# Token shift and value blocks moved by DMA, and one mask product per chunk, in a two-block transformer kernel

## The reference

```python
def shift_token(t):
    t1, t2 = jnp.split(t, 2, axis=-1)
    t2 = jnp.pad(t2, ((0, 0), (1, 0), (0, 0)))[:, :-1]
    return jnp.concatenate([t1, t2], axis=-1)
...
# first block
scores = jnp.einsum('bhqd,bhkd->bhqk', q, k) / math.sqrt(hd)
scores = jnp.where(causal_mask, jnp.finfo(scores.dtype).min, scores)
pattern = jax.nn.softmax(scores, axis=-1)
...
# second block, per layer
h = shift_token(x)
q, k, v = jnp.split(h @ wqkv, 3, axis=-1)     # then l2norm, scales, rotary
x = x + local_attention(q, k, v) @ wo
h = shift_token(x)
h = (h - mu) / jnp.sqrt(var + 1e-05) * lg + lb
a, g = jnp.split(h @ w1 + b1, 2, axis=-1)
x = x + (a * gelu(g)) @ w2 + b2
```

## Time and profile before

| | |
|---|---|
| time, median of 3 runs | 2481.74 us (2478.46 to 2484.01) |
| profiled execution | 2479.8 us, its span 2478.0 us |
| busy share of PE, DVE, ACT, POOL | 91%, 68%, 69%, 71% |
| length of a steady iteration of 16 slots | about 291 us |
| mean granted TensorE clock | 0.979 |

### The profile page before, as it was taken

The page is one execution under the profiler, slowest core; times in us unless marked ns, Lnnn a source line. Parts: engine busy times, 40 slices in busy tenths (PEclk is TensorE's granted clock), DMA queues, the critical chain, the costliest instruction groups (busy, mean ns, idle before and its releaser), DMA issues.

```text
span 2478.0 us, 59154 instructions
## 1 busy us (share of the span) xinstructions
PE 2243.9 (91%) x22208; PEld 1567.1 (63%) x22208; DVE 1675.2 (68%) x3612; ACT 1702.9 (69%) x2766; POOL 1771.1 (71%) x1615
## 2 busy tenths in 40 slices
PE   4888999999999999999999999999999999988887
PEld 1454666676666666666676666666666666665665
DVE  3666766777676776777667676677667766556653
ACT  1455677677777777767777776776777777776663
POOL 2117777786877868777777867777777877788883
PEclk9899999999999999999999999999999999999998
DMA  4221001110110110111011001011111100000000
GB/s 136 62 66 53 29 26 29 44 34 20 42 32 27 36 38 27 26 47 33 22 34 42 27 29 38 22 41 36 33 27 31 45 23 19 8 12 12 2 3 12
DMA packets 74966, 81.99 MB, mean 33 GB/s; under 512 B 7545, under 2 KB 64294, under 8 KB 74674
## 3 DMA queue, kind: packets, MB, share of 16 engines
q1 hardware_dynamic: 74674, 78.04, 11.0%
HBM read 56.26 MB, written 20.97 MB: 31 GB/s over the span
## 4 chain that ended last, share of the span: by engine, by line
PE 50%; ACT 18%; DVE 12%; issue 10%; POOL 8%; DMA 1%; SPq 0%; DVEq 0%; ACTq 0%; POOLq 0%
PE ps L540 8%; PE ps L633 6%; PE ps L825 4%; PE ps L588 4%; PE ps L573 3%; PE ps L700 3%; ACT PT L1188 3%; PE ps L739 3%; PE ps L553 3%; PE ps L722 2%; PE ps L816 2%; DVE ss L1027 2%; DVE nmax L976 2%; POOL inv L1407 2%; PE ps L687 2%
## 5 line engine op out<-in xcount | busy, mean ns | idle before, releaser
L976 DVE TENSOR_REDUCE nmax<-ps 128x1 f32<-128x512 f32 (+3 forms) x1024 | 471.6, 485 | 383.2 <-PE ps L575 380.4
L1188 ACT ACTIVATE PT<-ps 128x512 f32<-128x512 f32 (+1 forms) x768 | 407.0, 533 | 327.7 <-PE ps L590 323.3
L1407 POOL TENSOR_TENSOR inv<-ss,nhalf 128x16 f32<-128x16 f32 x128 | 378.7, 2959 | 322.3 <-DVE QN L1010 322.3
L573 PE MATMUL ps<-KA,QA 72*128 72x512 bf16 (+3 forms) x1024 | 290.2, 310 | 38.4 <-DVE nmax L976 33.1
L1396 POOL TENSOR_TENSOR RS<-RAW,rot 128x512 f32<-128x512 f32 x256 | 324.9, 1290 | 0.0
L1402 POOL TENSOR_TENSOR RC<-RC,RS 128x1024 f32<-128x1024 f32 x128 | 304.0, 2375 | 18.9 <-POOL RS L1396 1.3
L1385 POOL TENSOR_TENSOR RC<-RAW,rot 128x1024 f32<-128x1024 f32 x128 | 307.9, 2405 | 0.0
L588 PE MATMUL ps<-QA,KA 75*128 75x512 bf16 (+3 forms) x1024 | 285.6, 305 | 19.5 <-ACT PT L1188 15.4
L687 PE MATMUL ps<-wqkv,ZT 128*128 128x512 f32 x512 | 242.8, 597 | 0.0
L1246 ACT COPY V_odd<-ps 128x512 f32<-128x512 f32 x128 | 74.9, 585 | 217.1 <-PE ps L700 216.5
L1017 DVE TENSOR_REDUCE nm<-ps 128x8 f32<-128x1024 f32 x128 | 156.2, 1220 | 96.1 <-PE ps L722 95.1
(11 more groups left out here) (130 smaller groups left out, 5674.6 us busy)
## 6 DMA issues: line engine op xcount, KB each, us to landing
QA<-parts SPq DMA_DIRECT2D x192, 96.0 KB
KA<-parts SPq DMA_DIRECT2D x192, 96.0 KB
parts<-qkp SPq DMA_DIRECT2D x32, 384.0 KB, 5.5
X_next<-in_x SPq DMA_DIRECT2D x17, 256.0 KB, 2.9
X<-in_x SPq DMA_DIRECT2D x16, 256.0 KB, 3.0
x_kept<-X SPq DMA_DIRECT2D x16, 256.0 KB, 3.0
XR<-x_kept SPq DMA_DIRECT2D x32, 128.0 KB, 3.7
out<-XR SPq DMA_DIRECT2D x32, 128.0 KB, 1.9
```

Source lines behind the costliest of these rows:

```text
L573: pe.matmul(dst[:, c0:c0 + w], QA[e][0:QK_ROWS, h % UNIT, qt * P:(qt + 1) * P], KA[e][0:QK_ROWS, h % UNIT, 0:w], start=True, stop=False)
L976: ins = v.tensor_reduce(nmax[:, NT - 1 - r, h % H1:h % H1 + 1], for_max(i, x)[:, c0:c0 + w], AX.X, ALU.max, negate=True)
L1188: a.activation(PT1[:, h % UNIT, c0:c0 + w], for_exp(i, x)[:, 0:w], ACT.Exp, scale=SCALE1).then_inc(exped.sem, 1)
L1407: g.tensor_tensor(inv[:, :], ss[:, :], nhalf[:, :], ALU.pow).then_inc(inv_ready.sem, 1)
```

## The change

There are three edits. The two diagonal blocks of the chunk of two pieces get one mask product, with the mask read twice (a step of 0 over the block). The shift and corner products, DVE's copy and the two matrices go; SP moves 127 rows of `Z` by one partition into `XN` by DMA, and the first row by another, as soon as `z_acc` says so. ACT copies the values once, to `V_odd`, and SP fills both halves of `V_even` from it with two DMAs. With them some steps stand elsewhere: DVE takes the statistics of the shifted half after `norms` and the moments after `gate_up`; POOL makes the root after the rotary sum.

```diff
@@ PE, scores_max (scores_exp alike, with blocks 0 and 3)
                         pe.matmul(dst[:, c0:c0 + w], QA[e][0:QK_ROWS, h % UNIT, qt * P:(qt + 1) * P],
-                                  KA[e][0:QK_ROWS, h % UNIT, 0:w], start=True, stop=False)
-                        last = pe.matmul(dst[:, c0 + w - P:c0 + w], identb[:, :], causal[:, :],
-                                         start=False, stop=True)
-                    last.then_inc(scored.sem, 1)
+                                  KA[e][0:QK_ROWS, h % UNIT, 0:w], start=r == CHUNKS[c][0], stop=False)
+                    n = len(CHUNKS[c])
+                    diagonal = dst[:, c0 + w - n * P:c0 + w].rearrange("p (t x) -> p t x", x=P)
+                    pe.matmul(diagonal, identb[:, :], causal[:, :].unsqueeze(1).to_broadcast([P, n, P]),
+                              start=False, stop=True).then_inc(scored.sem, 1)
@@ SP
+                def move_values(m):
+                    sp.wait_ge(*past(v_ready.sem, v_ready.at(i, m + 1)))
+                    for n, rows in enumerate((slice(0, WIN), slice(WIN, P))):
+                        sp.dma_start(V_even[(m + n) % 2][rows, :, :], V_odd[rows, :, :]).then_inc(v_moved.sem, 16)
+                def shift_tokens(m):
+                    l, z, tt = place(m)
+                    dst = XN[m // HT % 2][:, m % HT, D // 2:D]
+                    sp.wait_ge(*past(z_acc.sem, z_acc.at(i, m + 1)))
+                    sp.dma_start(dst[1:P, :], Z[z][0:P - 1, tt, D // 2:D]).then_inc(shifted.sem, 16)
+                    first = Z[z][P - 1:P, tt - 1, D // 2:D] if tt else ident[0:1, D // 2:D]
+                    sp.dma_start(dst[0:1, :], first).then_inc(shifted.sem, 16)
...
+                    if tile_in(i, s - 1):
+                        shift_tokens(s - 1)
                     if s % 2 == 0:
...
+                    if tile_in(i, s + 1):
+                        move_values(s + 1)
@@ PE
-                    pe.wait_ge(*past(v_ready.sem, v_ready.at(i, m + 1)))
+                    pe.wait_ge(*past(v_moved.sem, v_moved.at(i, 2 * (m + 1))))
...
-                def shift_tokens(m):
-                    l, z, tt = place(m)
-                    pe.wait_ge(*past(z_acc.sem, z_acc.at(i, m + 1)))
-                    dst = m_ps[:, D:D + D // 2]
-                    mm = pe.matmul(dst, shift[:, :], Z[z][:, tt, D // 2:D], start=True, stop=(tt == 0))
-                    if tt:
-                        mm = pe.matmul(dst, corner[:, :], Z[z][:, tt - 1, D // 2:D], start=False, stop=True)
-                    mm.then_inc(sh_mm.sem, 1)
@@ DVE
                 def add_heads(m):
+                    v.wait_ge(*past(x_tr.sem, x_tr.at(i, m // HT - 1)))
                     v.wait_ge(*past(wo_mm.sem, wo_mm.at(i, m + 1)))
...
+                def shifted_tokens(m):
+                    l, z, tt = place(m)
+                    v.wait_ge(*past(shifted.sem, shifted.at(i, 2 * (m + 1))))
+                    v.bn_stats(stats[z][:, tt, 6:12], XN[m // HT % 2][:, m % HT, half:D]).then_inc(tile_stats.sem, 1)
@@ ACT
-                    a.copy(V_odd[:, :, 0:E2], heads)
-                    a.copy(V_even[m % 2][0:WIN, :, 0:E2], heads[0:WIN, :, :])
-                    a.copy(V_even[(m + 1) % 2][WIN:P, :, 0:E2], heads[WIN:P, :, :]).then_inc(v_ready.sem, 1)
+                    a.wait_ge(*past(v_moved.sem, v_moved.at(i, 2 * m)))
+                    a.copy(V_odd[:, :, 0:E2], heads).then_inc(v_ready.sem, 1)
@@ POOL
                         rotate_by_cos(s + 2)
+                    if tile_in(i, s + 2):
+                        rotate_by_sin(s + 2)
                     if tile_in(i, s - 1):
                         tile_root(s - 1)
-                    if tile_in(i, s + 2):
-                        rotate_by_sin(s + 2)
```

More of the change, by code:

```diff
@@ L192, in build @@
         band = sb("band", [P, 2, P], BF16)
-        shift = sb("shift", [P, P])
-        corner = sb("corner", [P, P])
         cos1 = sb("cos1", [P, S])
@@ L360, in build @@
         v_ready = count("v_ready", ITEMS)
+        v_moved = Landed(nc, ctx, "v_moved", 2 * ITEMS)
         s_mm = count("s_mm", ITEMS)
@@ L373, in build @@
         z_acc = count("z_acc", ITEMS)
-        sh_mm = count("sh_mm", ITEMS)
-        sh_ready = count("sh_ready", ITEMS)
+        shifted = Landed(nc, ctx, "shifted", 2 * ITEMS)
         tile_stats = count("tile_stats", ITEMS)
@@ L391, in build @@
         y_out = landed("y_out", LANES)
-        N_FIRST, N_CONST = 4, 12 + L * 7
+        N_FIRST, N_CONST = 4, 10 + L * 7
         N_MADE = LANES + 9
@@ L416, in _ @@
                 (causal_t[:, :], t["causal_t"]), (band[:, :, :], t["band"]),
-                (shift[:, :], t["shift"]), (corner[:, :], t["corner"]),
                 (wqkv[:, :, :], t["wqkv"].rearrange("l d n -> d l n")),
@@ L588, in scores_exp @@
                         pe.matmul(dst[:, c0:c0 + w], KA[e][0:ROWS, h % UNIT, kt * P:(kt + 1) * P],
-                                  QA[e][0:ROWS, h % UNIT, kt * P:S], start=True, stop=False)
-                        last = pe.matmul(dst[:, c0:c0 + P], identb[:, :], causal_t[:, :],
-                                         start=False, stop=True)
-                    last.then_inc(scored_t.sem, 1)
+                                  QA[e][0:ROWS, h % UNIT, kt * P:S], start=kt == CHUNKS[c][0], stop=False)
+                    n = len(CHUNKS[c])
+                    diagonal = dst[:, 0:c0 + P].rearrange("p (t x) -> p t x", x=P)[:, ::NT - 1, :]
+                    pe.matmul(diagonal, identb[:, :], causal_t[:, :].unsqueeze(1).to_broadcast([P, n, P]),
+                              start=False, stop=True).then_inc(scored_t.sem, 1)
                 def turn_maxima(s, u):
@@ L759, in tokens_over @@
                     if tile_in(i, s - 1):
-                        pe.wait_ge(*past(sh_ready.sem, sh_ready.at(i, s)))
+                        pe.wait_ge(*past(z_acc.sem, z_acc.at(i, s)))
                     else:
@@ L765, in turn_o @@
                     pe.wait_ge(*past(on_ready.sem, on_ready.at(i, m + 1)))
-                    pe.wait_ge(*past(sh_ready.sem, sh_ready.at(i, m)))
+                    pe.wait_ge(*past(z_acc.sem, z_acc.at(i, m)))
                     mlp_over(m)
@@ L853, in body @@
                     attention_step(s, 2)
-                    if tile_in(i, s - 1):
-                        shift_tokens(s - 1)
                     if tile_in(i, s):
@@ L1048, in tokens @@
                     l, z, tt = place(m)
-                    xn = XN[m // HT % 2][:, m % HT, half:D]
-                    v.wait_ge(*past(x_tr.sem, x_tr.at(i, m // HT - 1)))
-                    v.wait_ge(*past(sh_mm.sem, sh_mm.at(i, m + 1)))
-                    v.tensor_copy(xn, m_ps[:, D:D + half]).then_inc(sh_ready.sem, 1)
+                    v.wait_ge(*past(z_acc.sem, z_acc.at(i, m + 1)))
                     v.bn_stats(stats[z][:, tt, 0:6], Z[z][:, tt, 0:half])
-                    v.wait_ge(*past(sh_ready.sem, sh_ready.at(i, m + 1)))
-                    v.bn_stats(stats[z][:, tt, 6:12], xn).then_inc(tile_stats.sem, 1)
+                def shifted_tokens(m):
+                    l, z, tt = place(m)
+                    v.wait_ge(*past(shifted.sem, shifted.at(i, 2 * (m + 1))))
+                    v.bn_stats(stats[z][:, tt, 6:12], XN[m // HT % 2][:, m % HT, half:D]).then_inc(tile_stats.sem, 1)
                 def tile_moments(m):
@@ L1059, in tile_moments @@
                     v.wait_ge(*past(tile_stats.sem, tile_stats.at(i, m + 1)))
-                    if tile_in(i, m + 4):
-                        norms(m + 4)
-                    else:
-                        v.tensor_copy(spare[:, 0:1], nhalf[:, 0:1])
+                    v.tensor_copy(spare[:, 0:1], nhalf[:, 0:1])
                     v.bn_aggr(mv[z][:, tt, :], stats[z][:, tt, :]).then_inc(tile_mean.sem, 1)
@@ L1118, in body @@
                     attention_step(s, 3)
+                    if tile_in(i, s + 3):
+                        norms(s + 3)
                     if tile_in(i, s - 1):
-                        tile_moments(s - 1)
-                    elif tile_in(i, s + 3):
-                        norms(s + 3)
+                        shifted_tokens(s - 1)
                     if b:
@@ L1127, in body @@
                         heads_over_sum((s + 17) // 2)
+                    if tile_in(i, s - 1):
+                        tile_moments(s - 1)
                     if s % 8 == 2 and lives(i, 2):
@@ L1457, in constants @@
         "one_row": np.ones((1, HS), f),
-        "shift": np.eye(P, k=1, dtype=f), "corner": ((q == P - 1) & (k == 0)).astype(f),
         "ones": np.ones((SPLIT, UNIT * S), bf),
```

## The result

The changed kernel takes 2462.4 us (median of 6 runs, 2457.4 to 2470.0), the kernel before 2483.3 us beside it (6 runs, 2478.5 to 2485.2). The profiled execution took 2464.7 us, its span 2462.9.

A forecast was written before the change was run, and what follows sets the result against it. PE was taken to bound the middle, a ring through POOL, DVE and PE the tail. 21 + 5 + 14 + 9 + 2 + 3 - 5 = 49 us off 2479.8, plus 1.9 to the runs' median, gave 2432 us; range 2410 to 2495.

The forecast's parts named there:

- The landing: DVE's new wait for the shifted rows' DMA: 3.9 us from issue (1.6 to 5.5), 5 us charged for scatter.
- a late landing: Rival, 20%: 127 rows crawl through one engine, DVE then PE wait in odd slots; 2547 us at a 6.5 us landing.
- 127 rows spread over all engines: Rival: all engines share the rows, landing in 1.6 us, scatter charge goes, 2427 us; counted within the forecast's 62%.
- The value copies: Two ACT copies per tile go; a third of PE's 43.4 us of waits behind them gained, 14 us (0 to 43).
- The shift products: PE's shift and corner products go: 21 us gained in even slots, 5 in odd ones (0 to 49.6 for both).
- the order on POOL: POOL's variance wait between its rotary products goes, mostly into waiting for DVE; 9 us from earlier maxima parts (0 to 18.6).
- the sign I had named as the one against me: Iterations that stay at 291 us with every wait of PE longer, where about 285 was forecast.
- The mask product: On PE, one 256-column product replaces two of 128 columns, 512 pairs: 2 us gained (0 to 5).
- The tail: Last iteration's 16 tiles, at most 0.41 us each if POOL's wait goes: 3 us gained.
- The gain is given back: Rival, 18%: PE reaches its waits earlier and stands longer, exponentials late for other reasons; 14 us gained, about 2468.

The follow-up runs named there:

- root_first: The changed kernel with POOL's old order, the root of the variance between the two rotary products: 2478.9 us, 0.9994 of the kernel before.

## Why the prediction was wrong

*The landing*, on which I thought it all hung, was right: DVE goes on 3.94 us after the issue in the row above, against 3.9 taken, and waits 16.2 us for it in the changed kernel, 7 times, where I charged the path 5. By the Trainium skill's rule cited in the prediction, one engine takes the 127 rows, which gave 3.2 to 5.0 us; the trace agrees: the 127 packets start one behind the other every 0.014 us, and the last ends 3.12 us after the issue in the median. The rivals of a late landing and of 127 rows spread over all engines fell with it. But one support of it was misread: the share of 0.07 of the earlier trace rows says nothing of how many engines a load uses, for in that window the packets of the operand loads had hardly begun. From 1246 to 1247 us the share is 0.67 and from 1248 to 1249 it is 0.81.

*The value copies*: 14 us alone, 14 forecast, and that the two agree is in part luck. The engine and the waits were named rightly, but 36 us of them went and not a third of 43, and PE stood 13 us longer for DVE instead; without the clamp the same edit gives 26.

*The shift products* and *the order on POOL* (21 + 5 + 9, with 3 in the tail and -5 for the landing: 33 us) gave 3. This is the step that failed. The prediction said of POOL that the wait for the variance "goes" and "turns into a longer wait for DVE". It did, 154.7 to 23.0 us, but I valued the wait as pure loss and never asked what ran on another engine inside it. DVE's clamp did, directly behind its reduction; with POOL busy it stood 60 us more, and the MLP's products behind it. The steady iterations kept their 291 us, the sign I had named as the one against me. The price is measured: leaving the clamp out is worth 20 us before the change and 42 after, so the change lost 22 of the missing 31 us to it. That doesn't make the new order on POOL a loss by itself: beside DVE's new order it gave 16 us where 9 were taken (root_first). What the sum lacked is a term for DVE held by POOL.

The other 9 us are open in part. Without the clamp the shift gives 21 where 33 stood and the values 26 where 14 stood, and together, masks included, they give 40 and not the 47 of their sum. The sum also had no term for the loop's edge, where without the clamp the change takes 5 us more in four iterations (148.0 to 153.4) and the shift alone 10 (158.2). That would be most of the 12 that the shift lacks; the traces show it, and no run isolates it.

*The mask product*: 2 forecast, none measured, with or without the clamp.

*The tail*: 3 forecast, 1 in the two traces (227.2 to 226.2 us), one execution each. The last four tiles with the end, where DVE stands 3.7 us a tile for the landing, take 60.3 us against 59.5, so there the change gives nothing.

*The gain is given back*, the rival at 2468, came nearest in time. Its view that PE reaches waits earlier is right (29 us more for DVE, 13 for the local attention's exponentials). Its main reason is not: the first block's exponentials were to stay late, and their wait fell from 31.7 to 8.7 us. The largest part, the 22 us, is DVE held by POOL.

The row that told it stood in the profile before: the clamp's mean of 381 ns against the 0.17 us of the single ones in the earlier trace rows says that it already waited for something in some of its 128 executions.

## What to carry to other kernels

Before you remove an engine's idle time, look at what the other engines do in it: of DVE's and POOL's operations in particular, list the ones whose mean is well over their shortest. Where a small DVE operation on SBUF alone sits on the path beside a busy POOL, try another form of it (here a reduction over pairs, 847 to 186 ns and 34 us of the kernel). And where products leave the bounding engine, price the next engine's queue, not the products.

## What was not expected of the hardware

- An elementwise maximum of 128x16 in float32 on DVE lasts 0.17 us with POOL idle and 1.23 us when it is issued as POOL begins a product. In two traces all 157 long ones end 0.03 us behind the end of a POOL operation. Spacing the elements doesn't help (889 ns in the mean), a reduction of 128x32 to 128x16 isn't held (186), nor is the same operation on one element (154).
- A transfer of 127 rows of 256 bytes, with one row more behind it, lets DVE go on 3.9 us after its issue; its packets start one by one, every 0.014 us.
- Left in POOL's way, an operation of 0.17 us that runs 128 times cost 20 us of a kernel of 2480, and 42 us after an edit that touched neither it nor its data.
